# Token embedding of a language-model tower: gathers signalled tile by tile over four semaphores

## The reference

```python
tables = [head_weight.T[:5000], tail_weight_0.T, tail_weight_1.T]      # 256, 64 and 16 wide
projs = [head_weight_proj.T, tail_weight_proj_0.T, tail_weight_proj_1.T]
y = 0
for i in range(3):                                                     # cut-offs 0, 5000, 20000, 50000
    mask = (x >= l_idx) & (x < r_idx)
    emb = tables[i][jnp.where(mask, x - l_idx, 0)]
    y = y + jnp.where(mask[..., None], emb @ projs[i], 0.0)
h = y * 16.0
h = h + _L0_attn_ref(_layernorm(h), ...)                               # q = x @ Wq[i] + bq[i] comes first
```

## Time and profile before

| what | value |
|---|---|
| runs | 1238.48, 1228.54 and 1236.07 us |
| median of the 3 runs | 1236.07 us |
| profiled execution, span from the first to the last instruction | 1236.4 us |
| PE, DVE, ACT, POOL busy | 89%, 61%, 47%, 26% of the span |
| embedding up to the first query product | 0 to 34.34 us |

### The profile page before, as it was taken

The page is one execution under the profiler, slowest core; times in us unless marked ns, Lnnn a source line. Parts: engine busy times, 40 slices in busy tenths (PEclk is TensorE's granted clock), DMA queues, the critical chain, the costliest instruction groups (busy, mean ns, idle before and its releaser), DMA issues. The chain is left out here.

```text
span 1236.4 us, 16294 instructions
## 1 busy us (share of the span) xinstructions
PE 1099.6 (89%) x4826; PEld 719.3 (58%) x4826; DVE 757.8 (61%) x2088; ACT 580.1 (47%) x973; POOL 316.1 (26%) x316
## 2 busy tenths in 40 slices
PE   4899999999999999999999989868988778787882
PEld 3556557656665765676576566635545445476661
DVE  2577665785777578567758763657787765332221
ACT  2572563464356446535644634545656542033341
POOL 6030010011001001100301010332006573557775
PEclk9999999999999999999999989879989778899896
DMA  5300110220022211102430000377522215279897
GB/s 129 117 1 1 48 73 21 82 94 27 21 72 68 68 60 47 59 33 83 151 141 1 18 1 2 79 161 127 105 53 94 71 56 214 62 169 186 170 232 138
DMA packets 58452, 103.05 MB, mean 83 GB/s; under 512 B 10858, under 2 KB 38214, under 8 KB 58123
## 3 DMA queue, kind: packets, MB, share of 16 engines
q1 hardware_dynamic: 39227, 59.29, 17.9%
q0 software_dynamic: 19152, 42.92, 13.5%
HBM read 58.59 MB, written 53.00 MB: 90 GB/s over the span
## 5 line engine op out<-in xcount | busy, mean ns | idle before, releaser
L563 PE MATMUL b_ring<-left 128*128 128x256 f32 x960 | 212.1, 379 | 0.0
L553 PE MATMUL b_ring<-right,left 128*128 128x512 f32 x480 | 208.4, 592 | 0.0
L563 PEld LDWEIGHTS b_ring<-left 128*128 128x128 f32 x960 | 181.4, 190 | 25.0 <-issue 1.0
L1104 POOL TENSOR_TENSOR b_rstd<-b_veps,b_mhalf 128x4 f32<-128x4 f32 x31 | 36.7, 1185 | 560.1 <-DVE b_veps L1178 560.1
L553 PE MATMUL b_ring<-XT,b_wqkv 128*128 128x512 f32 x384 | 170.1, 592 | 0.0
L553 PEld LDWEIGHTS b_ring<-right,left 128*128 128x128 f32 x480 | 91.2, 190 | 114.8 <-issue 103.0
L853 ACT ACTIVATE left<-b_ring,b_cur 128x512 f32<-128x512 f32 x128 | 88.0, 687 | 65.4 <-PE b_ring L553 44.3
L553 PEld LDWEIGHTS b_ring<-XT,b_wqkv 128*128 128x128 f32 x384 | 71.6, 190 | 77.6 <-issue 76.9
L1290 DVE RECIPROCAL b_mixing<-b_mixing 128x1024 f32<-128x1024 f32 x16 | 104.8, 6553 | 0.5
L2085 ACT ACTIVATE a_ET<-a_pB 128x512 f32<-128x512 f32 x128 | 74.2, 595 | 44.5 <-PE a_pB L1835 43.2
L1769 POOL DMA_INDIRECT xe<-m_row,m_idx x84 | 82.7, 984 | 46.2 <-issue 28.2
(11 more groups left out here) (336 smaller groups left out, 1871.3 us busy)
## 6 DMA issues: line engine op xcount, KB each, us to landing
xe<-b_nil POOLq DMA_DIRECT2D x16, 1284.0 KB, 5.9
a_ET<-xe SPq DMA_DIRECT2D x32, 321.0 KB, 4.0
left<-in_w SPq DMA_DIRECT2D x8, 1024.0 KB, 5.4
x_wt<-in_wexp SPq DMA_DIRECT2D x16, 384.0 KB, 4.7
b_wqkv<-in_wqkv SPq DMA_DIRECT2D x4, 768.0 KB, 4.6
b_rows<-in_rows SPq DMA_DIRECT2D x8, 384.0 KB, 5.0
right<-qparts SPq DMA_DIRECT2D x16, 192.0 KB, 4.9
left<-qparts SPq DMA_DIRECT2D x16, 192.0 KB, 5.0
```

Of the source, the lines that this page charges most:

```text
L553: last = pe.matmul(bank[:, :], lhsT(k), rhs(k), start=(k == 0), stop=(k == n_k - 1))
L563: last = pe.matmul(bank[:, j * D:(j + 1) * D], src[:, k, tile], weights[:, k, :], start=(k == 0), stop=(k == n_k - 1))
L1104: pool.tensor_tensor(rstd[:, :], veps[:, :], mhalf[:, :], ALU.pow).then_inc(s_rs, 1)
```

## The change

The semaphore of a gather is no longer that of its chunk but that of its place in it: tile t adds 16 to `s_g[t % 4]`, so that each of the four semaphores is used once per chunk. To keep two gathers from being in flight on one semaphore, POOL waits from tile 4 on before each gather until that of tile t - 4 has landed. PE waits before the transposes of every tile for that tile's gather alone. `xn_transposed(0)` stands one tile earlier, after the products of tile 5. DVE waits for `h` tile by tile ahead of each `bn_stats`. SP waits on the fourth semaphore at 64, which tile 15 brings. An unused line (`tiles = ...`) is gone. All lines of PE's part move up by one or two numbers in the new file.

```diff
--- before.py
+++ after.py
@@ -274,7 +274,7 @@
         s_vec = sem("b_vec_loaded")
         s_ids = sem("e_ids_loaded")
         s_zero = sem("e_rows_zeroed")
-        s_g = [sem(f"e_gathered{c}") for c in range(NC)]
+        s_g = [sem(f"e_gathered{i}") for i in range(TPC)]
         s_t = sem("e_rows_transposed")
         s_tc = sem("e_rowsT_ready")
         s_y = sem("e_projected")
@@ -404,7 +404,7 @@
                     sp.wait_ge(s_full, products_before(NC - 1) + 3 * KD + NC * PER_STEP * (b - 1))
                 sp.dma_start(wqkv[:, :, :, :], a["wqkv"][bass.ds(b, 1), :, :, :].rearrange("b j (k p) n -> p (b j) k n", p=P)).then_inc(s_wqkv, 16)
                 if not wait:
-                    sp.wait_ge(s_g[NC - 1], 16 * TPC)
+                    sp.wait_ge(s_g[TPC - 1], 16 * NC)
                 if wait:
                     sp.wait_ge(s_full, products_before(NC) + NC * PER_STEP * (b - 1))
                 sp.dma_start(wo[:, :, :], a["wo"][bass.ds(b, 1), :, :].rearrange("b (k p) n -> p (b k) n", p=P)).then_inc(s_wo, 16)
@@ -493,8 +493,7 @@
         @block.tensor
         def _(pe):
             def rows_transposed(t):
-                if t % TPC == 0:
-                    pe.wait_ge(s_g[t // TPC], 16 * TPC)
+                pe.wait_ge(s_g[t % TPC], 16 * (t // TPC + 1))
                 if t:
                     pe.wait_ge(s_tc, t)
                 for k in range(3):
@@ -522,7 +521,7 @@
                         w = P if k < 2 else EW - 2 * P
                         last = pe.matmul(pY, rowsT[0:w, t % 2, k, :], proj[0:w, k, :], start=(k == 0), stop=(k == 2))
                     last.then_inc(s_y, 1)
-                    if t == TPC + 2:
+                    if t == TPC + 1:
                         xn_transposed(0)
                     if t % TPC == TPC - 1 and t + 1 < last_tile:
                         rows_transposed(t + 1)
@@ -1067,9 +1066,11 @@
                 if c < 2:
                     pool.wait_ge(s_zero, c + 1)
                 for t in range(c * TPC, (c + 1) * TPC):
+                    if c:
+                        pool.wait_ge(s_g[t % TPC], 16 * c)
                     pool.indirect_dma_start(
                         rows[:, t, :], None, a["table"][:, :], bass.IndirectOffsetOnAxis(ap=ids[:, t:t + 1].bitcast(U32), axis=0),
-                        bounds_check=CUTS[3] - 1, oob_is_err=False).then_inc(s_g[c], 16)
+                        bounds_check=CUTS[3] - 1, oob_is_err=False).then_inc(s_g[t % TPC], 16)
 
             def embedding_rstd(c):
                 pool.wait_ge(s_ve, c + 1 + (c == NC - 1))
@@ -1315,9 +1316,8 @@
                     bias_added(r + pair + NC * PER_STEP * l, a1, pair, rows1[:, 0, :], ring[(r + pair) % RING])
 
             def embedding_norm(c):
-                dve.wait_ge(s_eh, TPC * (c + 1))
-                tiles = slice(c * TPC, (c + 1) * TPC)
                 for j in range(TPC):
+                    dve.wait_ge(s_eh, TPC * c + j + 1)
                     last = dve.bn_stats(estats[:, j, :], h[:, c * TPC + j, :])
                 flink(last)
                 aggregated(flink, TPC, estats, emv, eveps[:, :], 1e-5).then_inc(s_ve, 1)
```

## The result

The changed kernel takes 1237.61 us in the median of 19 runs (1233.02 to 1245.81), the kernel before 1234.70 us in 19 runs beside it. The ratio is 1.0034, with a 95% interval of 1.0018 to 1.0050, so 2.2 to 6.2 us slower. The forecast was +2.1 us, 1238.2 us.

The account below looks back on a forecast made before the run. PE, busy 89% of the span, was taken as the bound, with POOL's gathers holding back chunk 0's power. Hidden gains 0, reordering +0.8 and clock +1.3 gave +2.1 us, 1238.2 us; range 1229 to 1244 us.

Parts of the forecast that it names:

- PE's head start and the statistics: Before chunk 0's power: PE starts 3.97 us earlier, tile-wise statistics save 1.05 us; both hidden by POOL, counted 0.
- POOL is late next: Chunk 0's power stays behind all sixteen gathers on POOL, cannot start before 27.47 us; no gain counted.
- The added waits: Twelve waits ahead of POOL's gathers are already satisfied and cost 0.1 us together.
- That rival: POOL's added waits cost up to 0.28 us each, 3.4 us before the power; +5.5 us, 1241.6 us, chance 12%.
- The reordering: Chunk 0's transposes on PE one tile earlier leave two tiles' work behind the data; query products 0.8 us later.
- The clock: PE's new wait of some 4 us before chunk 0's transposes lets its clock fall, costing 1.3 us.
- Its upper bound, 3.9 us: Most the clock could cost: all PE work from 30.4 us to the first query product at slow rates.
- the rival in which the clock stays low throughout: All PE work after the wait up to the first query product runs slow; +4.7 us, 1240.8 us, chance 10%.
- The Trainium skill's rule: A long wait in front of matmuls lets PE fall to half rate, so those behind it run cold.
- The rule's strict form, +4.7 us: Everything behind PE's wait up to the first query product at the slow rate: 0.8 + 3.9 us.
- The sum: Over the whole kernel: hidden gains 0, reordering +0.8, clock +1.3, giving +2.1 us.
- another position of the clock's falls: Falls later in the run could cost or return a microsecond or two; rival of no net clock loss, chance 20%.

Follow-up runs that it names:

- the waits alone: Changed kernel keeping only its new semaphores and POOL's twelve waits, PE again waiting for four gathers and chunk 0's transposes behind tile 6; first query product at 34.61 us.
- the order undone: Changed kernel with the transposes of chunk 0 back behind the products of tile 6; median 1230.07 us against 1233.28, ratio 0.9978.
- PE kept busy: Changed kernel with 30 unused transposes in PE's wait for the normalised chunk 0; ratios 0.9970 and 0.9980 to the kernel before, medians 1229.85 and 1229.73 us.
- the busy start: Changed kernel, chunk 0's transposes behind tile 6, its power behind tile 11's gather, 48 unused transposes ahead of PE's first tile; 1224.06 us against 1233.18, ratio 0.9932.
- the order alone: Kernel before with only the transposes of chunk 0 moved one tile earlier; first query product at 36.00 us.
- the power early: Changed kernel with the power of chunk 0 behind the gather of tile 13 in POOL's stream; first query product at 32.13 us.
- the power early and the order undone: Changed kernel with chunk 0's power behind the gather of tile 13 and its transposes behind tile 6; medians 1228.62 against 1235.21 us, ratio 0.9976.

## Why the prediction was right

*PE's head start and the statistics.* Forecast: start at 9.95, `e_veps` at 22.65. Measured: 9.97 and 22.80. The landing of the first gather was taken from the right row.

*POOL is late next.* Right, and it is the point of the case. The power was forecast at 27.5 to 27.9 us and came at 27.48. I had counted no gain for the gap of 0.28 us ahead of the power; all of it but 0.02 us went. The gap was DVE's after all.

*The added waits.* Forecast 0.1 us, measured 0: the last gather starts at 26.46 us in the changed kernel and with the waits alone, and at 26.51 us with the order undone (26.47 before). That rival is out.

*The reordering.* Forecast 4.7 us from the data to the query product, measured 4.60 to 4.66 in three kernels at full clock. With the power's 0.27 us given back, the order's part comes to 30.02 + 4.65 = 34.67 us, +0.3 us over before, where +0.8 was forecast. The size was off mainly because PE had the data at 30.02 and not at 30.4 us: the gap of POOL's, 0.27 us, and the 0.1 us for the waits make up nearly all of it.

*The clock.* Forecast +1.3 us, from the one wait of before of similar length. Measured 37.13, 36.33 and 36.11 less 34.67: +2.5, +1.7 and +1.4 us. The term was too small, by 0.1 to 1.2 us, and that it came so near is partly luck: in the row that it was taken from the clock fell only when PE was at work again (three transposes at 49.06 us took 0.55 us, near the 0.49 of full clock), while here the transposes right behind the wait were slow already (1.97 us for eight instead of 1.04). Its upper bound, 3.9 us, and the rival in which the clock stays low throughout were too large, since the clock rose again during the products of tile 6 or just after. The Trainium skill's rule (TensorE: Matmul & The Clock Gate, "Loop structure matters more than you think") agrees with the trace in kind: three looks with an idle time of 3.3 to 3.8 us all have the fall, those with 1.3 and 1.7 us have none there. Behind waits of about 3 us later in the kernel the fall comes in some looks and not in others. The rule's strict form, +4.7 us, did not come.

*The sum.* Query product +2.8, +2.0 and +1.8 us in three looks, +2.2 us on average, where +2.1 was forecast: the order's term was 0.5 us too large and the clock's on average 0.6 us too small, and that they cancel is luck. The medians say +2.9 and +4.2 us, and the two ratios, 1.0034 and 1.0038, mean +4.2 and +4.7 us with near ends of +2.2 and +2.1. So the forecast of +2.1 us is the size of the stretch and about half of what the ratios say of the whole. At 721 us the three looks are 2.71, 0.42 and 3.10 us later than the first look at before, on average as much as at the query product; what is missing is withheld clock, by the means above, and whether the change causes it behind 721 us stays open.

*What a trace of one execution is worth here.* The forecast said that another position of the clock's falls could cost or return a microsecond or two. Up to 721 us that was about right (2.7 us between the looks at the changed kernel). It was too small for the span: looks at the changed kernel spanned 1243.3, 1228.9 and 1234.8 us.

## What to carry to other kernels

Where two streams meet within some tenths of a microsecond (here 27.47 and 27.67 us), the profile names only the one that came last as the releaser; a change that speeds that one up gains at most the distance between them until the other has been moved as well, so look for the other's last instruction in its own stream. A wait that is moved ahead of ready work costs that work afterwards, and here the clock besides (0.3 us and 1.4 to 2.5 us): put on the in-order engine what is ready first, then the wait. For a change of a few microseconds in a millisecond, read the shift of one instruction right behind the changed stretch, use many runs for the sign, and compare their mean granted clock as well; the shift itself can change by 1 to 2 us at later waits, and the span of a single profile can mislead by five times the effect.

## What was not expected of the hardware

Spans of one kernel's profiles differ by up to 14.4 us (1243.3 against 1228.9), all but 2.3 us of it after 721 us, where PE has short waits and the clock falls behind some of them in one execution and not in the next.

From 780 to 900 us the granted clock was 0.87 in both looks at before and 0.87 to 0.88 in the three at the changed kernel, but 0.89 to 0.90 in the three with PE kept busy at 27 us, and 0.90 with the order undone and with the busy start. It was 0.87 too with the order alone and with the power early, and 0.89 with the waits alone and with the power early and the order undone, so it does not go with the unused transposes only. The code there is the same. The rows of before and of the kernel with the busy start:

```profile
780.00:900.00 120.00, 99.44 (x727) 63.19 (x728) 80.22 (x200) 69.48 (x138) 27.02 (x37) 0.87 0.63 121
```

```profile
780.00:900.00 120.00, 102.06 (x779) 63.58 (x777) 84.58 (x226) 73.12 (x144) 26.72 (x37) 0.90 0.65 123
```

That may be one place where the kernels with unused transposes are faster by more than their first stretch explains, but nothing here shows how a stretch at 30 us could reach one at 800 us, and single looks vary by more elsewhere: from 900 to 1000 us the two looks at before have 0.81 and 0.88, the three at the changed kernel 0.81 to 0.93. It was not tried further and stays open.
